# Mixture of experts: from every expert for every token to 23 sorted blocks of 128 rows

## The reference

```
xn = layernorm(x);  x = x + attention(xn) + moe(xn)       # layer 0, banded attention, 16 heads
xn = layernorm(x);  x = x + mamba(xn) + fp4_mlp(xn)       # layer 1, scan over the sequence
```

## Time and profile before

| what | us |
|---|---|
| median of 3 runs (1725.7 to 1731.26) | 1726.28 |
| the profiled execution | 1726.19 |
| its span, first to last instruction | 1724.1 |
| TensorE, VectorE busy | 1327.1, 1246.4 |
| ScalarE, GpSimd busy | 732.6, 675.8 |
| share of the chain that ended last: TensorE, VectorE | 48%, 27% |
| mean granted TensorE clock | 0.92 of 2.4 GHz |

### The profile page before, as it was taken

How to read it: one execution, slowest core, us unless ns; L and a number is a source line. 1 busy time by engine, 2 the same in 40 slices (tenths; PEclk the granted TensorE clock), 3 DMA queues, 4 the chain that set the end, 5 groups by cost and what they waited for, 6 DMA issues and landing times.

```text
span 1724.1 us, 27415 instructions
## 1 busy us (share of the span) xinstructions
PE 1327.1 (77%) x8730; PEld 822.9 (48%) x8762; DVE 1246.4 (72%) x2289; ACT 732.6 (42%) x1007; POOL 675.8 (39%) x534
## 2 busy tenths in 40 slices
PE   3499987768888788768887888768877898745564
PEld 2266665534444576434444676424444676311223
DVE  3544455668999874569999864569999873379974
ACT  3222142437666144347655244256654334333320
POOL 5100000017989030028988130038987120046624
PEclk7699999888999999889999999889999999869997
DMA  6120011014111030013110030023110030022200
GB/s 164 51 42 1 1 31 31 13 38 123 56 44 32 2 58 16 15 57 112 54 43 25 4 56 17 14 79 95 61 41 16 4 56 17 0 63 67 62 6 13
DMA packets 54852, 72.32 MB, mean 42 GB/s; under 512 B 8396, under 2 KB 25604, under 8 KB 54660
## 3 DMA queue, kind: packets, MB, share of 16 engines
q1 hardware_dynamic: 49696, 68.40, 15.1%
q10 hardware_dynamic: 5012, 2.12, 0.5%
HBM read 61.36 MB, written 9.04 MB: 41 GB/s over the span
## 4 chain that ended last, share of the span: by engine, by line
PE 48%; DVE 27%; issue 11%; ACT 5%; POOL 3%; DMA 3%; SPq 1%; ACTq 1%; DVEq 1%; POOLq 0%; PEldq 0%
PE ps L800 11%; DVE hs L1216 8%; PE ps L813 6%; PE ps L723 3%; DVE hc L1228 3%; PE ps L957 3%; PE ps L973 3%; DVE negmax L1281 3%; PE ps L871 3%; PE ps L959 3%; PE ps L872 2%; PE ps L714 2%; DVE x L1202 2%; PE ps L1003 2%; DMA ks<-parts_d 2%
## 5 line engine op out<-in xcount | busy, mean ns | idle before, releaser
L800 PE MATMUL ps<-xnT,w1T 128*128 128x512 f32 (+1 forms) x768 | 384.4, 620 | 71.3 <-DVEq L186 42.1
L448 POOL TENSOR_TENSOR dBu<-du,bs 128x512 f32<-128x512 f32 x256 | 325.5, 1276 | 159.9 <-DMA bs<-b_d 117.2
L1216 DVE TENSOR_TENSOR_SCAN hs<-ps,carry,dBu 128x512 f32<-128x512 f32 x256 | 320.5, 1268 | 22.4 <-POOL dBu L448 18.9
L606 ACT ACTIVATE ps<-delta,A_s 128x512 f32<-128x512 f32 x256 | 173.3, 688 | 210.3 <-DVE hs L1216 209.7
L813 PEld LDWEIGHTS ps<-w2T,hT 128*128 128x128 f32 (+1 forms) x1536 | 198.2, 201 | 119.5 <-DVE x L1202 77.3
L813 PE MATMUL ps<-w2T,hT 128*128 128x128 f32 (+1 forms) x1536 | 207.3, 288 | 44.5 <-DVE x L1202 44.5
L438 POOL TENSOR_TENSOR y<-y,hc 128x512 f32<-128x512 f32 x168 | 213.4, 1271 | 23.0 <-DVE hc L1228 22.9
L800 PEld LDWEIGHTS ps<-xnT,w1T 128*128 128x128 f32 (+1 forms) x768 | 130.1, 187 | 187.8 <-issue 150.5
L1191 DVE TENSOR_TENSOR hT<-sa,ps 128x512 f32<-128x512 f32 (+1 forms) x192 | 129.8, 676 | 82.1 <-PE ps L800 61.0
L632 ACT ACTIVATE pt<-ps 128x1024 f32<-128x1024 f32 x128 | 130.0, 1022 | 114.4 <-PE ps L959 114.4
L414 POOL COPY x<-x 128x1024 f32<-128x1024 f32 x4 | 4.1, 1036 | 441.0 <-DVEq L186 441.0
(11 more groups left out here) (220 smaller groups left out, 1974.9 us busy)
## 6 DMA issues: line engine op xcount, KB each, us to landing
bs<-b_d SPq DMA_DIRECT2D x128, 256.0 KB, 3.3
qs<-parts_d SPq DMA_DIRECT2D x144, 64.0 KB
ks<-parts_d SPq DMA_DIRECT2D x144, 64.0 KB
parts_d<-part SPq DMA_DIRECT2D x8, 768.0 KB, 3.6
st<-in_L_ffn_w SPq DMA_DIRECT2D x16, 128.0 KB, 5.8
x_in<-in_L_attn_x SPq DMA_DIRECT2D x4, 512.0 KB, 4.3
out<-res SPq DMA_DIRECT2D x4, 512.0 KB, 3.2
st<-in_L_ffn_w SPq DMA_DIRECT2D x8, 176.0 KB, 6.0
```

The costliest lines, as they stand in the source:

```text
L448: pool.tensor_tensor(dBu[g][n_ % 2][:, :], du[:, g, tb * HALF:(tb + 1) * HALF], bs[n_ % RING][:, :], ALU.mult)\
L606: act.activation(decay_bank(g), delta[:, g, tb * HALF:(tb + 1) * HALF], ACT.Exp, scale=A_s[:, g, n_:n_ + 1]).then_inc(S["dA_r"], 1)
L800: pe.matmul(bank((2, 6)[k % 2] if gate else k % 2)[0:m, :], w1T[:, k // 3, gate * F + f0:gate * F + f0 + m], xnT[:, BAND + tb * HALF:BAND ...
L1216: dve.tensor_tensor_scan(hs[g][:, :], decay_bank(g), dBu[g][n_ % 2][:, :], carry[:, g, n_:n_ + 1], ALU.mult, ALU.add).then_inc(S["h_s"], 1)
```

## The change

The experts are computed for chosen pairs only. In C, the tokens' two choices (`chosen`, `either`) are counted by a triangular matrix on TensorE into ranks (`rk_p`); VectorE turns them into a slot for each token and choice (`slot_i`), in which every expert starts at a multiple of 128, and a table `ei` of the expert of each block. 2048 pairs and at most 7 partly filled blocks give 23 blocks, always. GpSimd scatters the rows of `xn0` to their slots in DRAM (`xs_d`, 16 indirect DMAs). In M, SyncE reads for each block its expert from `ei` into a register and loads that expert's 576 KB of weights from DRAM (`we_d`, written once in the setup, with columns padded from 352 to 384) into a ring of four; rows come and go in groups of four blocks. A block's rows are transposed on TensorE and copied by ScalarE, then go through six `up` products of 128 columns, Silu, one gate product of 384 columns and three `down` products. Blocks are dealt to the 16 steps, one or two each (`blocks_at`). In T, GpSimd gathers each token's two rows (16 indirect DMAs), and VectorE accumulates them into `x0` after the first half of the attention. `score` and VectorE's accumulations in M go away.

```diff
+FP = 3 * P
+NBLK = 2 * N // P + EXPERTS - 1
+GRP = 4
+NGRP = (NBLK + GRP - 1) // GRP
+SLOTS = NGRP * GRP * P
+WRING = 4
+WROW = 2 * FP + 3 * P
...
+        def blocks_at(e):
+
+            return range((NBLK * e + 15) // 16, (NBLK * (e + 1) + 15) // 16)
...
+            sp.wait_ge(S["wpad"], 4)
+            for e in range(EXPERTS):
+                sp.wait_ge(S["st_cp"], 3 * e + 3)
+                sp.dma_start(we_d[e], wst[:, e, :]).then_inc(S["we_out"], 16)
+            for g in range(NGRP):
+                sp.dma_start(xs_d[g * GRP * P:(g + 1) * GRP * P, :].rearrange("(s p) d -> p s d", p=P), zz[:, :, :]).then_inc(S["xz"], 16)
+            sp.wait_ge(S["we_out"], 16 * EXPERTS)
+            sp.wait_ge(S["xz"], 16 * NGRP)
...
+            def load_weights(b0, j):
+
+                if j >= WRING:
+                    sp.wait_ge(S["dn_b"], b0 * NBLK + j - WRING + 1)
+                    settle(sp)
+                e = sp.value_load(ei[0:1, j:j + 1], min_val=0, max_val=EXPERTS - 1)
+                sp.dma_start(wb[j % WRING][:, :], we_d[bass.ds(e, 1), :, :].rearrange("o p c -> p (o c)")).then_inc(S["wb_in"][j % WRING], 16)
...
                 if b0 is not None:
+                    sp.wait_ge(S["ei_r"], b0 + 1)
+                    settle(sp)
+                    for j in range(WRING):
+                        load_weights(b0, j)
+                    sp.wait_ge(S["sc_out"], b0 * 256 + 256)
+                    settle(sp)
+                    for g in range(2):
+                        load_rows(b0, g)
...
+                for e in range(16):
+                    if b1 is not None:
+                        for t in (2 * e, 2 * e + 1):
+                            if t + RING < 2 * NST:
+                                load_b(b1, t + RING)
+                    if b0 is not None:
+                        for j in blocks_at(e):
+                            if j + WRING < NBLK:
+                                load_weights(b0, j + WRING)
+                            if j % GRP == 0 and j // GRP + 2 < NGRP:
+                                load_rows(b0, j // GRP + 2)
+                            if j % GRP == 2 and j > GRP:
+                                store_rows(b0, j // GRP - 1)
+                if b0 is not None:
+                    store_rows(b0, NGRP - 1)
+                    for r in range(2):
+                        sp.wait_ge(S["ys_out"][r], (b0 + 1) * 16 * (NGRP // 2))
+                        settle(sp)
...
+                    pool.wait_ge(S["slot_r"], b0 + 1)
+                    settle(pool)
+                    for k in range(2):
+                        for i in range(TILES):
+                            pool.indirect_dma_start(out=xs_d, out_offset=bass.IndirectOffsetOnAxis(ap=slot_i[:, k, i:i + 1], axis=0),
+                                                    in_=xn0[:, i, :], in_offset=None).then_inc(S["sc_out"], 16)
...
+                if b0 is not None:
+                    for k in range(2):
+                        for i in range(TILES):
+                            pool.indirect_dma_start(out=yg[:, k, i, :], out_offset=None, in_=ys_d,
+                                                    in_offset=bass.IndirectOffsetOnAxis(ap=slot_i[:, k, i:i + 1], axis=0)).then_inc(S["yg_in"], 16)
...
+                def silu(j):
+
+                    v = b0 * NBLK + j
                     act.wait_ge(S["a_p"], v + 1)
-                    act.wait_ge(S["h_r"], nth("h_r", v - 4))
-                    act.activation(sa[k % 4][0:m, :], bank(k % 2)[0:m, :], ACT.Silu).then_inc(S["sa_r"], 1)
+                    if j >= 2:
+                        act.wait_ge(S["h_r"], v - 1)
+                    act.activation(sa[j % 2][:, :], bank(j % 2)[:, 0:FP], ACT.Silu).then_inc(S["sa_r"], 1)
...
+                for e in range(16):
+                    if b0 is not None:
+                        for j in blocks_at(e):
+                            silu(j)
+                            if j % GRP == 2 and j // GRP + 1 < NGRP:
+                                rows_turned(j // GRP + 1)
+                            if j % GRP == 1 and j > GRP:
+                                rows_done(j // GRP - 1)
                     for n_ in range(2 * e + 1, min(2 * e + 3, 2 * NST)):
                         decay(n_, 0)
                         decay(n_, 1)
...
+                if b0 is not None:
+                    pe.wait_ge(S["m_r"], b0 + 1)
+                    pe.wait_ge(S["v_r"], b0 * 3 + 3)
+                    o = bank(6)[:, 0:(TILES + 1) * EXPERTS].rearrange("p (i e) -> p i e", e=EXPERTS)
+                    pe.matmul(o[:, 0:TILES, :], before[:, :], either[:, :, :], start=True, stop=False, skip_group_check=True)
+                    for i in range(TILES):
+                        t = pe.matmul(o[:, i + 1:, :], ones_b[:, :], either[:, i:i + 1, :].broadcast_to([P, TILES - i, EXPERTS]),
+                                      start=False, stop=(i == TILES - 1), skip_group_check=True)
+                    t.then_inc(S["rk_p"], 1)
...
+                def up(j, gate):
+
+                    v = b0 * NBLK + j
                     if gate:
-                        pe.wait_ge(S["h_r"], nth("h_r", v - 2))
+                        if j:
+                            pe.wait_ge(S["h_r"], v)
...
+                        pe.wait_ge(S["wb_in"][j % WRING], (b0 * loads_of(j % WRING) + j // WRING + 1) * 16)
+                        pe.wait_ge(S["xT_r"], b0 * NGRP + j // GRP + 1)
+                        if j >= 2:
+                            pe.wait_ge(S["sa_r"], v - 1)
+                    o = bank(2 if gate else j % 2)
+                    for c in range(3):
+                        t = pe.matmul(o[:, c * P:(c + 1) * P], wb[j % WRING][:, gate * FP + c * P:gate * FP + (c + 1) * P],
+                                      xT[j // GRP % 2][:, j % GRP * P:(j % GRP + 1) * P], start=True, stop=True)
+                    t.then_inc(S["g_p" if gate else "a_p"], 1)
...
+                def block(j):
+
+                    if j == 0:
+                        turn_rows(0)
+                    if j % GRP == 2 and j // GRP + 1 < NGRP:
+                        turn_rows(j // GRP + 1)
+                    up(j, 0)
+                    if j:
+                        down(j - 1)
+                    up(j, 1)
...
+                    todo = blocks_at(e) if b0 is not None else ()
+                    if todo:
+                        block(todo[0])
                     spread_c(2 * e + 1)
                     add(2 * e)
-                    up(3 * e + 2, 1)
-                    if e:
-                        down(e - 1, 2)
-                        down(e - 1, 3)
-                    up(3 * e + 4, 0)
-                    up(3 * e + 5, 0)
+                    for j in todo[1:]:
+                        block(j)
...
+                if b0 is not None:
+                    dve.wait_ge(S["rk_p"], b0 + 1)
+                    o = bank(6)[:, 0:(TILES + 1) * EXPERTS].rearrange("p (i e) -> p i e", e=EXPERTS)
+                    link0(dve.tensor_scalar(nblk[:, :], o[:, TILES, :], 1.0 / P, 0.5 - 0.5 / P, ALU.mult, ALU.add))
+                    link0(dve.tensor_scalar(nblk[:, :], nblk[:, :], 2.0 ** 23, 2.0 ** 23, ALU.add, ALU.subtract))
+                    link0(dve.tensor_tensor_scan(upto[:, :], ones8[:, :], nblk[:, :], 0.0, ALU.mult, ALU.add))
+                    link0(dve.tensor_tensor(base[:, :], upto[:, :], nblk[:, :], ALU.subtract))
+                    link0(dve.scalar_tensor_tensor(out=place[:, :, :], in0=base[:, :].unsqueeze(1).broadcast_to(s3), scalar=float(P),
+                                                   in1=o[:, 0:TILES, :], op0=ALU.mult, op1=ALU.add))
+                    for k in range(2):
+                        link0(dve.tensor_tensor(chosen[k][:, :, :], chosen[k][:, :, :], place[:, :, :], ALU.mult))
+                        link0(dve.tensor_reduce(slot_f[:, k, :], chosen[k][:, :, :], AX.X, ALU.add))
+                    dve.tensor_copy(slot_i[:, :, :], slot_f[:, :, :]).then_inc(S["slot_r"], 1)
...
+                    dve.tensor_copy(ei[:, :], ei_f[:, :]).then_inc(S["ei_r"], 1)
...
+                for e in range(16):
+                    todo = blocks_at(e) if b0 is not None else ()
+                    for t, mine in ((2 * e, todo[:1]), (2 * e + 1, todo[1:])):
+                        scan(t, 0)
+                        scan(t, 1)
+                        times_c(t, 0)
+                        for j in mine:
+                            times_g(j)
+                        times_c(t, 1)
...
+                    if s == 0 and b0 is not None:
+                        dve.wait_ge(S["yg_in"], b0 * 256 + 256)
+                        for k in range(2):
+                            for i in range(TILES):
+                                t = dve.scalar_tensor_tensor(out=x0[:, i, :], in0=yg[:, k, i, :], scalar=pwt[:, k, i:i + 1],
+                                                             in1=x0[:, i, :], op0=ALU.mult, op1=ALU.add)
```

(17 more changed lines are left out.)

227 lines of the change are left out of this document (108 added, 119 removed).

## The result

The changed kernel takes 1856.0 us (median of 4 runs, 1847.5 to 1857.3); the kernel before, run beside it, 1726.0. The ratio is 1.074 (95% interval 1.070 to 1.078): slower by 130 us, where 73 were forecast. The profiled execution took 1857.2, its span 1855.4.

A forecast was written before the change was run, and what follows sets the result against it. TensorE bounds the first M; VectorE the shared M at 10.16 us a step, GpSimd just behind. 15 + 18.5 - 36 + 1 + 3 x (11.4 + 10 + 3.5) = +73 on 1726 gives 1799 us, range 1740 to 1875.

The forecast's parts named there:

- Setup: Before the first C: row DMAs wait for stores of transposed experts and zeros, losing their cover; +15 us.
- Scatters: End of C: 16 issues on GpSimd at 1.24 us each lie on the path; +11.4 each shared C, +18.5 first.
- or if sections C don't grow: The prediction's own sign against itself: it is wrong if the sections C do not get longer.
- Shared M, start: Shared M before its second step: rows land behind weights, block 0 delays the scans; 29.1 us instead of 15.6, +14.
- `bs` load 4: Shared M, SyncE: lands about 11 us later than 23.5, but step 2, needing it, starts 14 later; costs nothing.
- Shared M, steps: Shared M, steps 1 to 15: two-block steps 11.9 us, one-block 7.8, GpSimd's need 148.8; 151 against 152.4, -1.4.
- ScalarE's order decides: Two-block steps of shared M: both Silu precede the second scan pair's decay; scan starts at 7.9 us, not 4.1.
- The half clock: Rival: bursts leave TensorE at half clock, 12 us more each shared M; with slow weight loads, 1832 to 1835; chance 0.15.
- Tail: End of each shared M: the last accumulations fall away; -3 us.
- T: Attention after M: gathers hidden, VectorE's 16 accumulations take 4.5 us before a needed maximum; +3.5 in three, +1 in the first.
- the dear scatters: Rival, end of C: GpSimd's scatters cost 2.12 us each, 1855 us in all; chance 0.22.
- GpSimd's floor: Rival, shared M: Silu chain hidden and rows early, GpSimd's operations bound the stage at 166 us; 1721 in all; chance 0.12.

The follow-up runs named there:

- e4: Changed kernel with setup's row DMAs issued before the zero stores and waits, and T's additions moved into the maxima loop: 1832.9 us, 1.066 of the kernel before.
- e3: Changed kernel with 14 of a batch's 16 scatters left out, so most sorted rows stay zero: 1832.3 us, 1.063 of the kernel before.
- e1: Changed kernel with extra TensorE matmuls that nobody reads in every expert stage: 1836.1 us, 1.066 of the kernel before.
- e8: Changed kernel with decays before second Silu, later blocks and scatters, additions among maxima, zero stores first, extra matmuls in shared M: 1703.5 us, 0.988 of the kernel before.
- e2: Changed kernel with ScalarE running a two-block step's first two decays before the second Silu and row copies: 1774.3 us, 1.029 of the kernel before.
- e10: Changed kernel with the second expert rank's eight scatters left out, eight of sixteen staying: 1845.9 us, 1.070 of the kernel before.

## Why the prediction was right and wrong

*Setup* (+15 forecast, +14.6): right, the row DMAs began at 43.75 behind the wait. By e4 the wait's cause is the last store to land, whichever it is.

*Scatters* (1.24 us each; measured 1.28 on average in the first C, 1.42 in the shared C): near in price, wrong in place. The step that failed here is "as section C ends only when every engine has come to the barrier, these lie on the path". GpSimd came to the barrier ahead of its own issues. By the prediction's own sign ("or if sections C don't grow") its account is refuted for the shared C. The first C grew by 5.9 instead of 18.5 and the shared C by nothing to speak of; the first M paid part of it (-30.0 instead of -36; the two together -24 against -17.5 forecast): its rows, forecast to land at 11 us, landed at 16.7 behind the scatters, and at 10.4 without them (e3). In the shared M the issues lay beside other waits and were worth 4 us (e3). The 1 us that the Trainium skill gives ("DMA: Bandwidth & Descriptors", Latency and other measured facts) is for the first byte, which no row shows; the 0.97 us of an issue is near it, its spacing of 1.27 is not.

*Shared M, start* (second step at 29.1 us forecast; 31.5, 31.0, 31.7): right to 2.6 us. One link was another: the rows landed at 16.7 instead of 14.7, held by the scatters and not by the weights; without the scatters the weights hold them to 14.4 (e3). And `bs` load 4, which was to land in time and cost nothing, landed at 42.8, 40.4 and 35.1 us against 34.5 forecast; VectorE waited 3.6 and 1.8 us behind it in the first two stages.

*Shared M, steps* (-1.4 forecast, +22.1 to +22.9 measured from the second step to the last pair of scans): this is the term that failed, and with it the size of the forecast. It named the right order ("ScalarE's order decides") and priced it at full clock: 7.9 us for the first half of a two-block step, 4.1 for that of a one-block step. Measured in the first shared M: 9.0 to 13.2 and 5.2 to 7.2. With a warm TensorE (e1) the best halves came to 8.0 and 4.1, so the arithmetic held where its clock did. The half clock stood among the rivals at 12 us a stage and 0.15; e1 measured 13.4. The evidence against it, full clock at 53% busy, was one window of four microseconds; in a stage where each pass waits for VectorE or ScalarE in turn, TensorE was busy 47% of the time and granted 0.66. What the forecast lacked beside the clock were the gate products' waits in the steps (24.3 us in the first shared M, costed at nothing; the 6.3 at the start were in its sum) and the copies of rows that stand in ScalarE's queue with the Silus. The waits for decays, 31.7 us, would be 7 x 3.8 = 26.6 by the forecast's own halves; that they show in the time, rather than vanish under GpSimd's 148.8, is put down to the rest being late as well (GpSimd was busy 74% of the stage), which is argued and not shown.

*Tail* (-3 forecast): -2.6.

*T* (+3.5 forecast, +12): the additions and a slower start. The 16 additions took 7.02 us, not 4.5, and e4 shows them on the path (in the first T, with no GpSimd work beside them, they took 4.41). And T now begins at the low clock: TensorE was granted 0.50 in the first 4 us of the first shared T, 1.00 before the change, and there the second maximum came 4.20 us after the first instead of 2.19 (VectorE before, the first two rows, and in the changed kernel):

```profile
572.07 1.22 DVE L1281 TENSOR_REDUCE negmax<-ps 128x4 f32<-128x1024 f32 x1 [1.68 <-PE ps L872]
...
574.26 1.22 DVE L1281 TENSOR_REDUCE negmax<-ps 128x4 f32<-128x1024 f32 x1
...
606.50 1.23 DVE L1423 TENSOR_REDUCE negmax<-ps 128x4 f32<-128x1024 f32 x1 [2.56 <-PE ps L1028]
610.70 1.23 DVE L1423 TENSOR_REDUCE negmax<-ps 128x4 f32<-128x1024 f32 x1 [1.04 <-PE ps L1028]
612.88 1.23 DVE L1423 TENSOR_REDUCE negmax<-ps 128x4 f32<-128x1024 f32 x1
...
672.50 7.02 DVE L1498 SCALAR_TENSOR_TENSOR x<-yg,pwt,x 128x128 f32<-128x128 f32 x16
679.66 1.22 DVE L1423 TENSOR_REDUCE negmax<-ps 128x4 f32<-128x1024 f32 x1
```

That is 2.0 us, and 0.9 more in front of the first maximum (1.4 in all in the second T); in e1, with passes up to the end of M, the spacing is 2.19 again, though T as a whole got back only 1.7 us or nothing. The last 2 of the 12 us lie at the mark: before, VectorE began the next C 2.7 us after the load that marks it, now 0.3. The first T grew by 4.1 against 1 forecast; moving the additions (e4) took 1.0 off it, and the rest is not shown.

*The sum.* In the profiled executions, where the change is 131 us, C was forecast too dear by 44, the shared M too cheap by 78, T (all four, with what follows the last) by 19, the first M by 6. The forecast's direction and range held because errors of both signs met, and that is luck: with C as measured the same sum gives 1755. Of the rivals, the clock was real as a part; the dear scatters gave 1855, the measured time, for a reason that was false, which a single time could not have told. GpSimd's floor, 166 us, is what e8 comes near to with 10 us of scatters added.

## What to carry to other kernels

When work is cut on an engine that others wait for in turn, price the new chain at the clock that it will itself be granted (here the low one for two thirds of the stage), and ask of each in-order queue what stands behind an instruction that can now be late. A short edit of one queue's order (e2) was worth more than any wait removed elsewhere. An end-of-section barrier tells that an engine's queue was passed on, not that its issued DMAs are done, so look for their cost in the next section.

## What was not expected of the hardware

A barrier behind GpSimd's indirect DMAs passed after 0.40 us an issue, while the engine worked them off 1.27 us apart (e10). VectorE's additions of 0.34 us took 1.76 and 1.54 where they ran beside GpSimd's operations of 1.68 and 1.39 at 672.44 and 674.19, which is the 2.6 us between 7.02 and 4.41. And matmuls that nobody reads made a stage shorter: 344 more passes in the first shared M (e1) raised the granted clock from 0.66 to 0.80 and took 13.1 us off it.
